# Heads h and h+8 as pairs, doubled score stacks with fewer transfers, and output copies a unit later in three attention stages

## The reference

```python
# "rms": q and k normed per head
q = _rmsnorm(q, wq); k = _rmsnorm(k, wk)
attn = softmax(einsum('bqhd,bkhd->bhqk', q, k))
x = x + (einsum('bhqk,bkhd->bqhd', attn, v).reshape(b, s, d) @ Wo.T + bo)
# "decay": causal, with a second product of lines, weighted by distance
logits = std_logits + incidence * weights * bias_scale
# "relative": a bias by distance and head
scores = einsum('bhqd,bhkd->bhqk', q, k) + compute_bias(rel_emb, S, S)
```

## Time and profile before

| | |
|---|---|
| three runs | 6170.70, 6177.96, 6174.44 us; median 6174.44 |
| profiled execution | 6174.04 us, its span 6172.2 us |
| mean granted clock of TensorE | 0.882 |
| busy over the span | PE 81%, DVE 59%, ACT 53%, POOL 23% |
| stage rms | first exp 47.7 us, last 713.0 us |
| stage decay | first exp 1299.1 us, last 2306.2 us |
| stage relative | first exp 2810.2 us, last 3494.4 us |

### The profile page before, as it was taken

One profiled execution on the slowest core, in us unless ns is written; L12 is line 12 of the kernel. 1 busy time (PEld: TensorE's weight loads), 2 busy tenths in 40 slices (PEclk: granted clock), 3 DMA queues, 4 the chain that ended last, 5 costly groups with the idle time before them and its releaser, 6 DMA issues. The chain is left out here.

```text
span 6172.2 us, 94930 instructions
## 1 busy us (share of the span) xinstructions
PE 5010.2 (81%) x30276; PEld 2497.9 (40%) x30276; DVE 3641.6 (59%) x6830; ACT 3287.2 (53%) x5223; POOL 1392.0 (23%) x1261
## 2 busy tenths in 40 slices
PE   6898859488888785977888838699999999999657
PEld 2222459433333334962222425333434334334435
DVE  4333465556566567547777773276666666765662
ACT  5888625324444451536888603466666665665212
POOL 0000127423233321751222128200000000000147
PEclk8999869778888895988999858899999999999668
DMA  2211122312222222222211213200000000000213
GB/s 79 62 54 56 54 45 49 79 37 80 75 69 79 73 63 52 50 71 63 60 55 54 68 37 55 53 1 0 0 0 0 0 0 0 0 0 0 64 26 50
DMA packets 232980, 264.59 MB, mean 43 GB/s; under 512 B 35557, under 2 KB 192965, under 8 KB 232684
## 3 DMA queue, kind: packets, MB, share of 16 engines
q1 hardware_dynamic: 198514, 219.78, 12.9%
q0 software_dynamic: 34176, 40.86, 3.8%
HBM read 164.05 MB, written 96.06 MB: 42 GB/s over the span
## 5 line engine op out<-in xcount | busy, mean ns | idle before, releaser
L1330 DVE TENSOR_TENSOR slot_decay<-slot_decay,dtab_decay 128x1024 f32<-128x1024 f32 (+3 forms) x512 | 418.8, 830 | 302.9 <-PE slot_decay L826 288.0
L2712 ACT ACTIVATE prob_wide<-slot_wide 128x1024 f32<-128x1024 f32 x512 | 494.0, 1016 | 149.6 <-PE slot_wide L2611 149.6
L997 ACT ACTIVATE prob_decay<-slot_decay 128x1024 f32<-128x1024 f32 (+3 forms) x512 | 354.4, 706 | 397.5 <-PE slot_decay L846 396.7
L997 ACT ACTIVATE prob_relative<-slot_relative 128x1024 f32<-128x1024 f32 x512 | 498.0, 1058 | 55.8 <-PE slot_relative L841 54.2
L997 ACT ACTIVATE prob_rms<-slot_rms 128x1024 f32<-128x1024 f32 x512 | 491.5, 1052 | 60.4 <-PE slot_rms L841 60.2
L2611 PE MATMUL slot_wide<-qT_wide,kT_wide 64*128 64x512 f32 x2048 | 508.8, 615 | 2.9 <-ACT prob_wide L2712 2.9
L1341 DVE TENSOR_TENSOR prob_relative<-prob_relative,rtab_relative 128x1024 f32<-128x1024 f32 (+1 forms) x256 | 396.2, 1553 | 157.0 <-ACT prob_relative L997 149.1
L2624 PE MATMUL obank_wide<-prob_wide,v_wide 128*64 128x512 f32 x2048 | 467.7, 598 | 1.8 <-DVE zT_wide L2774 1.8
L2077 POOL TENSOR_TENSOR xn_choice_b<-X,stats_choice_b 128x512 f32<-128x512 f32 x8 | 8.4, 1048 | 1892.7 <-DVEq L2259 1892.7
L864 PE MATMUL obank_relative<-prob_relative,vaug_relative 128*32 128x512 f32 x2048 | 283.7, 627 | 89.0 <-DVE prob_relative L1341 86.0
L2760 DVE TENSOR_TENSOR sums_wide<-sums_wide,prob_wide 128x1024 f32<-128x1024 f32 x256 | 313.7, 1225 | 28.7 <-ACT prob_wide L2712 0.2
(11 more groups left out here) (839 smaller groups left out, 10556.0 us busy)
## 6 DMA issues: line engine op xcount, KB each, us to landing
scratch_decay<-parts_decay SPq DMA_DIRECT2D x192, 128.0 KB, 2.4
scratch_rms<-parts_rms SPq DMA_DIRECT2D x96, 128.0 KB, 2.4
kst_rms<-scratch_rms SPq DMA_DIRECT2D x192, 64.0 KB
kst_decay<-scratch_decay SPq DMA_DIRECT2D x192, 64.0 KB
kin_decay<-scratch_decay SPq DMA_DIRECT2D x192, 64.0 KB
scratch_relative<-parts_relative SPq DMA_DIRECT2D x96, 128.0 KB, 2.3
kst_relative<-scratch_relative SPq DMA_DIRECT2D x192, 64.0 KB
qst_rms<-scratch_rms SPq DMA_DIRECT2D x64, 128.0 KB
```

The source lines that it names most:

```text
L997: nc.scalar.activation(prob[:, Q % 2, p:G:2, at:at + m], slot[:, u % 3].rearrange("p (k c) -> p k c", k=2)[:, :, 0:m], ACT.Exp).then_inc(e ...
L1330: nc.vector.tensor_tensor(sl, sl, dtab[:, head(g, p):head(g, p) + G + 1:G, 0:m], ALU.mult).then_inc(biased, 1)
L2712: nc.scalar.activation(prob[:, Q % 2, u % 4, :], slot[:, u % 2, :], ACT.Exp).then_inc(exp_done, 1)
```

## The change

`narrow_attention` is changed for rms and relative. The old function stays under the name `decay_attention` and is called for decay; in it only decay's lag goes from 1 to 2.

In the changed function a pair is head h and head h+8. Both stacks hold two buffers, each for all 16 heads; block b reads one and the transfers for block b+1 write the other. Since the heads of one half of the partitions are now the heads 0 to 7 in a row, and 8 to 15 of the other, one transfer fills a whole row range: 10 per block in rms and 12 in relative, each with twice the data of one before. The constant of three rows is no longer sent in rms. One semaphore counts them, and S waits for it once a block instead of at units 0 and 16. In relative, eight transfers at the start instead of six put the constant rows into both buffers. Indices of the tables, of z and of the bias follow the new pairs, with the same instructions. The plans change in four places.

```diff
 "rms":
-    lnexp=12, o3=11, z=13, y=23, turn=(17, 20), mid=1, o=(15, 25, 30), lag=1, lead=1
+    lnexp=12, o3=11, z=13, y=23, turn=(15, 17), mid=1, o=(19, 25, 30), lag=2, lead=1
 "relative":
-    turn=(11, 14), mid=1, o3=17, z=19, y=23, o=(21, 25, 30), lag=2, lead=1
+    turn=(11, 14), mid=1, o3=17, z=19, y=23, o=(21, 25, 30), lag=3, lead=1
 "decay" (in decay_attention):
-    o=(18, 25, 30), lag=1, lead=0
+    o=(18, 25, 30), lag=2, lead=0
-qst = sb("qst", [P, H // 2, S], BF16)
-kst = sb("kst", [P, H // 2, S], BF16)
+qst = sb("qst", [P, 2, H // 2, S], BF16)
+kst = sb("kst", [P, 2, H // 2, S], BF16)
 def head(g, j):
-    return G * (g - g % 2) + 2 * (g % 2) + j % 2 + G * (j // 2)
+    return 2 * g + j % 2 + H // 2 * (j // 2)
-def stack(f, l, side):
+def stack(buf, side):
     for k in range(2):
-        heads = slice(2 * G * f + G * k, 2 * G * f + G * k + G)
+        heads = slice(H // 2 * k, H // 2 * (k + 1))
 ...
-        if l == 0 and side == 0:
-            sp.dma_start(st[half_rows(k, KR, KS), to, :], no_shift).then_inc(stacked[f], 16)
+        if relative and side == 0:
+            sp.dma_start(st[half_rows(k, KR, KS), buf], no_shift).then_inc(stacked, 16)
 STACK, after the six scratch writes:
-for f in range(1 if l < NL - 1 else 2):
-    ...
-            if m == 0 and side == 0 and not at_start(b, -1):
-                sp.wait_ge(s_filled, at["used", f])
-            stack(f, m, side)
+if not (at_start(b, -1) or at_start(b, 0)):
+    sp.wait_ge(s_filled, at["used"])        # b * UNITS: the last block's scores
+for side in range(2):
+    sp.wait_ge(scr_written[side], at["written"])
+    stack(1 - buffer[0], side)
 S on PE:
-if u % (UNITS // 2) == 0:
-    pe.wait_ge(stacked[g // 2], (b + 1) * STACKED)
+if u == 0:
+    pe.wait_ge(stacked, (b + 1) * STACKED)
```

More of the change, by code:

```diff
@@ L213, in narrow_attention, with decay_attention @@
+def decay_attention(nc, sem, A, X, kind, NB, w, x_in=None, safe=SAFE):
     rms, decay, relative = kind == "rms", kind == "decay", kind == "relative"
@@ L382, in narrow_attention @@
             "decay": dict(line=(3, 4), qkv=(6, 7, 8, 9), cross=5, norms=9, root=(13, 15), lnexp=14, ext=16, size=17,
-                          turn=(12, 14, 19, 21), mid=1, o3=10, z=16, y=23, peak=22, bound=24, o=(18, 25, 30), lag=1,
+                          turn=(12, 14, 19, 21), mid=1, o3=10, z=16, y=23, peak=22, bound=24, o=(18, 25, 30), lag=2,
                           lead=0),
@@ L2799, in model @@
                 wp="L0_ffn_wp", w2="L0_ffn_wo"), "top2_a", 0),
-            lambda: narrow_attention(nc, sem, A, X, "decay", NB, dict(
+            lambda: decay_attention(nc, sem, A, X, "decay", NB, dict(
                 wqkv="L0_attn_b_w_qkv", bqkv="L0_attn_b_b_qkv", wo="L0_attn_b_w_out", bo="L0_attn_b_b_out",
```

1096 lines of the change are left out of this document (added).

## The result

The changed kernel takes 6161.25 us (median of 17), the kernel before 6186.23 in the same comparison: ratio 0.996, interval 0.9948 to 0.9973. The forecast was 6115, from 6082 to 6152, so the gain was real and less than half of what I had said. Its profiled execution has a span of 6159.9 us and a mean clock of 0.887.

A forecast was written before the change was run, and what follows sets the result against it. No engine was at its limit in the three stages; waits at joins counted. From 6174.0 us, rms -68, decay -24, relative +33 and its start -1 gave 6114, taken as 6115, range 6082 to 6152.

The forecast's parts named there:

- The transfers of rms: Rms's stack lands 35.6 us after the block's first scores, so PE's wait of 3.1 us a block goes.
- rival (d): Doubled transfers cost more per issue, the stack stays late and rms gains nothing: 6183 us; chance 0.06.
- the 1.8 us of slack: Rms's stack at 35.6 us would be 1.8 us early for a next block beginning at 37.4 at the earliest.
- The clock: In rms the clock falls behind each block's stack wait would go with it, 1.7 of 2.1 us a block.
- Rival (c): Rms keeps its clock falls or a rest of the wait, +13 to +26: 6128 to 6141 us; chance 0.17.
- The period without the wait: A block of rms falls from 42.0 to 37.5 us, -63 over fourteen periods; rms as a whole -68.
- Decay: The later copy takes 1.6 us a block off PE's waits for ACT in product I: -24, between 0 and -39.
- Relative: Later copies delay PV, +1.1 at group 3 and +1.1 at groups 1 and 2: +33, between -19 and +52.
- my three places: In relative, PV delays of 1.3 us at group 3, 1.65 at group 1 and 0.55 at group 2.
- Rival (a): The later copy costs relative nothing, since PE waits for bands anyway: 6082 us; chance 0.15.
- Relative's start: Tables come 7 us earlier but the eight far transfers end about the same time: -1, between -4 and +1.

The follow-up runs named there:

- e3: Changed kernel, but rms sends its stacks in two halves with rows of 4096 bytes and S waits for each half; 6137.03 us, ratio 0.9921.
- e5: Changed kernel, but each of rms's ten stack transfers carries only four of its eight heads; 6262.14 us in one execution, kernel before 6323.1.
- e4: Kernel before with only rms's new plan (turn at 15 and 17, o at 19, 25, 30, lag 2); 6138.49 us, ratio 0.9917.
- e7: Changed kernel with rms's stacks sent in halves and relative's lag back at 2; 6228.44 us, ratio 0.9849 to the kernel before.
- e10: Changed kernel with rms's stacks sent in halves and rms's lag back at 1; 6155.25 us in one execution, kernel before 6207.72.
- e15: Changed kernel with rms's stacks sent in halves, run once more; 6268.30 us, ratio 0.99 to the kernel before.
- e16: Changed kernel with rms's stacks in halves; in relative, copy of group 3 at lag 2 and TURN_Z at 20; 6235.98 us, ratio 0.9861.
- e11: Changed kernel with rms's stacks in halves and rms's turn back at 17 and 20; 6133.93 us in one execution, kernel before 6207.72.
- e6: Changed kernel, but each rms stack transfer is cut in two by rows, 20 transfers in all; one execution, rms block 46.3 us.
- e9: Changed kernel, but in rms two k transfers of 16 rows become one of 32; 6262.05 us in one execution, kernel before 6207.72.
- e2: Changed kernel with decay's lag back at 1; 6206.97 us, ratio 1.0039 to the kernel before.
- e8: Changed kernel, but in relative the copy of group 3 is back at lag 2, the others at 3; 6267.91 us, ratio 0.9912.
- e13: Changed kernel, but rms's k scratch is laid out so that four k transfers each read 16 neighbouring DRAM rows; 6297.97 us, ratio 0.9977.

## Why the prediction was wrong

**The transfers of rms, the step that failed.** "10.7 to 11.5 us after the last part is split" the stack was to be complete, of which 2.1 to 3.0 us of landing. The landing was 6.3 us; it is the term that failed. I had the warning in the sum: 190 GB/s at a share of 0.65 I scaled to 292 GB/s at a full share and set 5.4 us against the issue. That stretch held scratch writes of 1024-byte packets beside the stack's. The transfers in question had been seen only at 98 GB/s, the rate of their issues, so no row bounded their drain, and I gave its upper end 3.0 us. The 358 GB/s that the Trainium skill gives per core ("DMA: Bandwidth & Descriptors", section "Specifications") are a limit of the memory and were no price of these transfers: they drained at 131. The issues took 6.9 us, 0.3 over the forecast and without growth in size, so rival (d) was wrong in its mechanism. ("Six writes of 1.9 us" are the three writes behind the last part, 0.60 each; the sum is right with them.)

A second step was short as well: the last part was split 26.5 us after the block's first scores on average, not 24.8, and in e3, without any fall of the clock, just as late. So the 1.8 us of slack were not there. Together: 1.7 us from the split, 0.3 from the issues and 4.0 from the landing put the stack at about 41.6 us instead of 35.6, while PE was ready at 38.8; that is the wait of 2.8 us, with its fall of the clock. The split alone costs no wait, as e3 and e5 show, whose rows have 4096 bytes, and e4 with the old transfers. Of rival (d) the outcome for rms is nearly right, a gain of 3 to 12 us instead of none, with another cause.

**The clock.** Right where it could be tested: with the wait goes the fall. The mean clock of the rms stage is 0.99 in every run without the wait (e3, e4, e5, e7, e10, e15, e16), 0.94 to 0.96 with it, also in e11, and 0.90 and 0.89 in e6 and e9, where the wait is longest. What the Trainium skill says of it ("TensorE: Matmul & The Clock Gate", section "HAM oscillation — how this bites in real kernels"), a throttling behind each wait for a DMA, agrees with this. Rival (c) asked for falls that stay when the wait has gone, and that did not occur; in the changed kernel both stayed.

**The period without the wait.** 38.35 instead of 37.5 (e3, e4, e5 alike). The wait of 3.1 us went and PE was busy 1.8 us less a block (500.45 instead of 525.15 in 14), as forecast, but other waits of PE grew by 1.7 where I had 0.3: 1.05 for DVE's xn at a block's start, 0.8 for the output copies, 0.4 for DVE's normed qk, and less for ACT's exps. Over 14 blocks that is 588 to 544 us, -44, where I had -63; it would have been a size error only.

**Decay.** The wait came out as forecast: PE waits 1.7 us less a block for ACT's exp, where I had 1.6, so -24 was right for what it priced. The stage gained 44, since two things that I had no term for moved too: PE was busy 8 us less in 14 blocks (736.44 to 728.42, clock 0.87 to 0.88), and its other idle time shrank by 11. e2, where only the lag differs, has 46 us in the whole time and 52 in the 14 blocks, 35 of them by the clock; its ten executions have a mean clock of 0.880 to 0.883, the 17 of the changed kernel 0.882 to 0.891. So the lag moves the clock; by what path stays open. By eight runs with lag 2 and rms undivided against three with lag 1 (1008 to 1021 us) the stage is 54 us shorter.

**Relative.** +28.4 against +33: 1.1 for group 3 as forecast (e8), 0.7 to 0.9 for the others (1.1 forecast). Each wait that I had worked out was there within 0.15 us. The near hit hides two larger terms: PE waits 5.0 us a block for the four copies, where my three places add up to 3.5, and against it stand 1.3 us less of waits for the bands and 1.1 us less of busy time (473.80 to 459.80 in 13 blocks, clock 0.98 to 1.00). Rival (a) is refuted.

**Relative's start.** -1 against +4.1. The tables, on which I had the start wait, were not last; the eight far transfers were. Their first issue waits for DVE's casts, of which ownk's is 1.06 us longer with twice the data (2.28 instead of 1.22), their issues last 8.3 us instead of 5.8, and the scores start 5.0 us after the last. I had let them end together with the tables. From the end of the scratch writes to the first scores that is 1.9 of the 4.1 us; the other 2.2 lie earlier and are not explained.

## What to carry to other kernels

The time of a DMA issue says nothing on its drain: 0.65 us for 64 and for 128 KB, with a landing of 2.1 and of 6.3. When a change makes transfers larger at the same pitch, look for a stretch of the trace in which just these transfers are queued, and if there is none, carry the drain as an unknown with a wide bound; send first only the part that the next step needs. When a step is moved by a unit in an in-order list, see which other instruction comes to stand in front of it: there it was zT. With the copy of group 3 back at its place and zT moved too, a loss of 1.9 us a block became a gain of 0.7. And when a wait goes as forecast and the stage still gains twice as much, look at the busy time and the clock before calling the mechanism right.

## What the runs showed of the hardware

In these runs a transfer from DRAM to SBUF kept as many DMA engines busy as the outermost dimension of its source had entries: 2 (e9, share 0.14), 4 (e6, 0.25), 8 (changed kernel, 0.51), 16 (e13, about 1.05). For the k transfers of 16 rows more engines did not help: rows of 8192 bytes took 0.32 us with 4 engines at work, 0.51 with 8, and up to 1.4 us with 16, and over ten microseconds 8 and 16 engines moved 129 and 125 GB/s. The end of q, with a double copy of 32 rows in it and up to 16 rows on their way at once, reached 205 GB/s at 0.46 us a row. An issue of a k transfer took 0.65 us with 64 or 128 KB, and 0.43 once its 16 rows lay in a row in DRAM (e13).

Decay's matmuls kept PE busy 788 us at a mean clock of 0.91 (e7) and 848 at 0.84 (e16), for a stage of 946 and 1002 us. Within one execution of the changed kernel blocks of 62 us at 0.91 and of 68 us at 0.81 occur.
